# Graph network kernel: message types applied to a whole round of 16 groups at once, with VectorE's additions one round later

## What is computed

```python
h = jax.nn.relu(node_features @ node_proj_w.T + node_proj_b)
for l in range(L):                                   # L = 2
    trans = jnp.einsum('nh,tdh->tnd', h, edge_W[l])  # 8 types, 128 x 128 each
    msgs = trans[edge_type, src]
    agg = jax.ops.segment_sum(msgs, dst, num_segments=num_nodes)
    h = jax.nn.relu(_gru_cell(agg, h, gru_wih[l], gru_whh[l], gru_bih[l], gru_bhh[l]))
return h @ out_w.T + out_b
```

## Time and profile before

| | us |
|---|---|
| median of 3 runs | 2032.73 |
| lowest, highest | 2016.99, 2032.94 |
| profiled execution | 2030.53 |
| its span, first to last instruction | 2028.7 |
| mean granted clock | 0.897 of 2.4 GHz |
| PE busy | 1533.5 (76%) |
| POOL busy | 1189.5 (59%) |
| DVE busy | 809.0 (40%) |
| ACT busy | 500.7 (25%) |

### The profile page before, as it was taken

How to read it: one execution, slowest core, us unless ns; L and a number is a source line. 1 busy time by engine, 2 the same in 40 slices (tenths; PEclk the granted TensorE clock), 3 DMA queues, 4 the chain that set the end, 5 groups by cost and what they waited for, 6 DMA issues and landing times.

```text
span 2028.7 us, 32940 instructions
## 1 busy us (share of the span) xinstructions
PE 1533.5 (76%) x10492; PEld 1061.7 (52%) x10493; DVE 809.0 (40%) x3350; ACT 500.7 (25%) x958; POOL 1189.5 (59%) x1282
## 2 busy tenths in 40 slices
PE   5467888787778865777774888888887776677786
PEld 3345555454545544666562545555555445556565
DVE  6657262524323244454443222222523224444443
ACT  5233151514225112222221101111514211122221
POOL 7355666566556664666634666665665565566661
PEclk9679999899899977898987999989998987899998
DMA  6423727163462422222213776765243362222221
GB/s 165 125 58 110 238 85 269 54 235 118 137 201 68 136 75 65 80 78 78 76 50 103 257 239 226 257 217 152 68 133 88 90 170 64 68 75 71 75 76 32
DMA packets 183323, 251.61 MB, mean 124 GB/s; under 512 B 24396, under 2 KB 156641, under 8 KB 183201
## 3 DMA queue, kind: packets, MB, share of 16 engines
q1 hardware_dynamic: 123041, 130.73, 20.5%
q0 software_dynamic: 58176, 119.22, 20.3%
q10 hardware_dynamic: 1984, 0.13, 0.1%
HBM read 211.87 MB, written 38.12 MB: 123 GB/s over the span
## 4 chain that ended last, share of the span: by engine, by line
PE 39%; another core or an unknown queue 27%; issue 11%; DVE 10%; DMA 4%; ACT 4%; DVEq 3%; SPq 1%; POOL 1%; PEld 1%; ACTq 0%; PEldq 0%; POOLq 0%
PE ps L1070 11%; PE ps L1141 7%; PE ps L1047 7%; PE ps L1133 5%; PE ps L1008 4%; DMA blocks<-node_table 3%; PE ps L1121 3%; DVE acc L1653 2%; DVE onehot L1576 2%; ACT counts L775 2%; PE ps L1113 1%; ACT sums_sb L845 1%; PE ps L1086 1%; DVE acc L1673 1%
## 5 line engine op out<-in xcount | busy, mean ns | idle before, releaser
L587 POOL DMA_INDIRECT gath<-node_table,srcT x1212 | 1153.5, 952 | 793.2 <-issue 305.6
L1673 DVE TENSOR_TENSOR acc<-ps,acc 128x16 f32 x864 | 150.7, 174 | 785.3 <-remote 338.4
L1070 PE MATMUL ps<-counts,blocks 128*128 128x504 f16 (+3 forms) x1764 | 413.4, 381 | 63.9 <-issue 31.6
L845 ACT COPY sums_sb<-ps 128x512 f32<-128x512 f32 x216 | 126.2, 586 | 829.7 <-remote 514.6
L1070 PEld LDWEIGHTS ps<-counts,blocks 128*128 128x128 bf16 x1764 | 169.8, 100 | 257.6 <-issue 75.3
L1047 PE MATMUL ps<-work 128*128 128x392 bf16 x983 | 218.1, 357 | 110.2 <-ACT counts L775 43.6
L1141 PE MATMUL ps<-sums_sb,wT 128*128 128x128 f32 x1728 | 244.4, 299 | 65.2 <-ACT sums_sb L845 55.7
L1141 PEld LDWEIGHTS ps<-sums_sb,wT 128*128 128x128 f32 x1728 | 230.6, 212 | 82.9 <-DVE acc L1673 30.0
L1133 PE MATMUL ps<-onehot,gath 128*128 128x128 bf16 x2592 | 200.7, 228 | 59.3 <-issue 39.3
L1133 PEld LDWEIGHTS ps<-onehot,gath 128*128 128x128 bf16 x2592 | 174.8, 103 | 103.1 <-issue 66.0
L775 ACT CAST counts<-ps 128x392 f16<-128x392 f32 x429 | 187.7, 498 | 118.8 <-PE ps L1047 52.4
(11 more groups left out here) (199 smaller groups left out, 869.8 us busy)
## 6 DMA issues: line engine op xcount, KB each, us to landing
blocks<-node_table SPq DMA_DIRECT2D x84, 672.0 KB
kept_counts<-counts SPq DMA_DIRECT2D x28, 882.0 KB
counts<-kept_counts SPq DMA_DIRECT2D x28, 882.0 KB
gath<-node_table,srcT POOLq DMA_INDIRECT x1212
node_table<-gath SPq DMA_DIRECT2D x14, 336.0 KB, 3.2
node_table<-work SPq DMA_DIRECT2D x14, 336.0 KB
counts<-in_x_dram SPq DMA_DIRECT2D x1, 3080.0 KB
out_dram<-counts SPq DMA_DIRECT2D x13, 224.0 KB
```

The source lines that it names most:

```text
L587: nc.gpsimd.indirect_dma_start(out=gath[:, b, j, :], out_offset=None, in_=tables[l], in_offset=bass.IndirectOffsetOnAxis(ap=index, axis=0) ...
L845: act.copy(n_sb[:, b // 2, b % 2 * BG:(b % 2 + 1) * BG, :], narrow_sums[b % 2]) \
L1070: last = nc.tensor.matmul(head_ps[:, 0:COLS[share]], blocks[:, j % 2, at, part * H:(part + 1) * H], counts[:, a, 0:COLS[share]], start=(i ...
L1673: nc.vector.tensor_tensor(win, narrow_ps[q][:, g * NARROW:(g + 1) * NARROW], win, ALU.add) \
```

## The change

The types are applied less often, in wider products, and DVE's additions move.

- Narrow rounds: all four slots' sums are copied side by side into one place (`n_sb`, now a single place and not two halves), and `narrow_types` runs once, at the end of the round, with 256 columns. DVE makes the 16 additions at the start of the next round (`add_narrow(n - 1)`), before it writes one-hots; the one-hots of a slot now wait for `sums_ready` of that slot, and `make_hots` for the head stands behind the one-hots of slots 1 and 3.
- Wide rounds: a new `wide_types` covers two slots with 192 columns; it runs after slot 2's sum and after slot 3's. DVE adds 8 windows in a row (`add_wide`), then writes two slots' one-hots, then runs the tile's piece. `before_tanh` stands first in DVE's round.
- The short last round keeps `by_type`.

```diff
-        win_ps = [ps[:, 4 + b, 0:BG * WIN] for b in range(2)]
-        narrow_ps = [ps[:, 4 + q, 0:2 * BG * NARROW] for q in range(2)]
+        win_ps = [ps[:, 4 + q, 0:2 * BG * WIN] for q in range(2)]
+        narrow_ps = ps[:, 4, 0:ROUND * NARROW]
...
+                def wide_types(k, q):
+                    pe.wait_ge(es[l]["sums_copied"], k + (2 * q + 4))
+                    pe.wait_ge(es[l]["acc_added"], (k + 2) * BG)
+                    for t in range(T):
+                        last = nc.tensor.matmul(win_ps[q].rearrange("p (g w) -> p g w", g=2 * BG),
+                                                wT[:, W_EDGE + l * T + t, :],
+                                                s_sb[:, q, :, t * WIN:(t + 1) * WIN],
+                                                start=(t == 0), stop=(t == T - 1))
+                    last.then_inc(es[l]["win_done"], 2)
...
-                def narrow_types(k, q):
-                    pe.wait_ge(es[l]["sums_copied"], k + (2 * q + 4))
-                    pe.wait_ge(es[l]["acc_added"], (k + 2 * q) * BG)
+                def narrow_types(k):
+                    pe.wait_ge(es[l]["sums_copied"], k + (SLOTS + 2))
+                    pe.wait_ge(es[l]["acc_added"], (k + 2) * BG)
...
                     narrow_sums_of(k, landed, 2)
                     if head is None:
                         piece(pe, begin, gate_in, l + 1, tile)
-                    narrow_types(k, 0)
-                    if head is None:
                         piece(pe, begin, gate_z, l + 1, tile)
...
                     sum_by_code(k, landed, 0)
                     sum_by_code(k, landed, 1)
                     piece(pe, begin, gates_begin, k, tile)
-                    by_type(k, 0)
+                    sum_by_code(k, landed, 2)
                     piece(pe, begin, gate_in, l + 1, tile)
-                    sum_by_code(k, landed, 2)
-                    by_type(k, 1)
+                    wide_types(k, 0)
                     piece(pe, begin, gate_z, l + 1, tile)
                     sum_by_code(k, landed, 3)
-                    by_type(k, 2)
-                    by_type(k, 3)
+                    wide_types(k, 1)
                     piece(pe, begin, to_rows, l + 1, tile)
...
                 def narrow_round(n, head=None, last=False):
                     if head is None:
                         begin, tile = round_tile(dve, mybir.EngineType.DVE, n)
+                        add_narrow(n - 1)
+                    elif head > 0:
+                        add_narrow(n - 1, added_until(l, head))
                     k = n * SLOTS
+                    for b in range(SLOTS):
+                        dve.wait_ge(sem_l["sums_ready"], k + (b + 1 + SLOTS))
+                        (one_hots if last else narrow_hots)(n * ROUND + (ROUND + b * BG), b)
+                        if head is not None:
+                            if b % 2:
+                                for g in MADE[l].get(head + b - 1, []):
+                                    make_hots(g)
+                            head_slot(l, head + b, (k + 2) * BG)
+                        elif b == 1:
                             piece(dve, begin, before_tanh, l + 1, tile)
+                        elif b == 2:
                             piece(dve, begin, new_state, l + 1, tile)
+                        elif b == 3:
                             piece(dve, begin, state_parts, l + 1, tile)
```

More of the change, by code:

```diff
@@ L311, in gnn_kernel @@
         hots = onehot.rearrange("p b g c -> p (b g c)").bitcast(F32)
-        places = (one_half[0:ROWP, 0, 0:RC * GE], one_half[0:ROWP, 1, 0:RC * GE], hots[0:ROWP, 0:RC * GE])
+        places = (one_half[0:ROWP, 0:RC * GE], one_half[0:ROWP, RC * GE:2 * RC * GE], hots[0:ROWP, 0:RC * GE])
         dst_i, src_i, typ_i = (rows(t, I32) for t in places)
@@ L843, in narrow_round @@
                         act.wait_ge(es[l]["sums_ready"], k + (b + 1 + SLOTS))
[L844 to L845 removed]
+                        if b == 0:
+                            act.wait_ge(es[l]["win_done"], k + 2)
+                        act.copy(n_sb[:, b * BG:(b + 1) * BG, :], narrow_sums[b % 2]) \
                            .then_inc(es[l]["sums_copied"], 1)
@@ L1654, in add_windows, with add_wide @@
                           .then_inc(sem_l["acc_added"], 1)
-                def add_narrow(k, g0, q, after_head, hots):
-                    if len(hots) <= FIRST_HOTS:
-                        for g in hots:
-                            make_hots(g)
-                        hots = []
+                def add_wide(k, g0, q):
                     for half in range(2):
@@ L1680, in narrow_round @@
                         begin, tile = round_tile(dve, mybir.EngineType.DVE, n)
+                        add_narrow(n - 1)
+                    elif head > 0:
+                        add_narrow(n - 1, added_until(l, head))
                     k = n * SLOTS
[L1682 to L1693 removed]
+                    for b in range(SLOTS):
+                        dve.wait_ge(sem_l["sums_ready"], k + (b + 1 + SLOTS))
[6 more added lines that the diff above has]
+                        elif b == 1:
+                            piece(dve, begin, before_tanh, l + 1, tile)
+                        elif b == 2:
                             piece(dve, begin, new_state, l + 1, tile)
[L1695 removed]
+                        elif b == 3:
                             piece(dve, begin, state_parts, l + 1, tile)
```

89 lines of the change are left out of this document (43 added, 46 removed).

## The result

The changed kernel took 2050.24 us (median of 20 runs), the kernel before 2027.45 (20 runs): ratio 1.0124, 95% interval 1.0099 to 1.0149. It is slower by 1.2%, and inside the range of 1960 to 2085, but the forecast was "no change", 2026 us, and the time lies above the forecast's own range of 2005 to 2045. The profiled execution's span is 2047.2 us, 18.5 more than before.

A forecast was written before the change was run, and what follows sets the result against it. A signal loop of PE, POOL and ACT was taken as the bound. Head -29, narrow +18 and wide +4 gave -7 on 2030.5, 2023.5 us; 2.2 for the median made 2026. Own range 2005 to 2045, with rivals 1960 to 2085.

The forecast's parts named there:

- the charge for the late signal in the wide rounds: Wide rounds: new_state waits behind eight additions begun by a late first-types signal, charged 2.3 us a round.
- What bounds the kernel: All rounds: a loop of PE, POOL and ACT through signals; results during gather runs seen up to 5 us late.
- Head rounds, "I take -0.6, the work alone": 48 head rounds: one 256-column types call replaces two of 128, saving 0.6 us each, -29 us in all.
- the rule of the Trainium skill: Head types: loads priced at columns over 1.2 GHz, 107 ns; by it the change saves nothing, head term 0.
- Narrow rounds with a tile, "I take +3": Six narrow rounds with a tile: additions in line before the gates, less part of the types, +18 us in all.
- Wide rounds, +0.2: Twenty wide rounds: four parts sum to -2.1 us, against a late-signal charge of 2.3; +4 us in all.
- part (2): Wide rounds: before_tanh comes first on DVE, removing PE's wait before gate_z, -2.9 us a round.
- part (1): Wide rounds: two types calls of 192 columns replace four calls, 7.7 to 5.2 us, -2.5 us a round.
- the second: Slower rival, 2076 us: DVE becomes the spine of rounds with a tile, +2.5 us a wide round; chance 0.24.
- The first: Faster rival, 1967 us: loops loosen, one POOL idle per head round goes, wide rounds gain; -66 us, chance 0.33.
- The third: Slower rival, 2075 us: late head one-hots make PE wait about 3 us in 17 counting rounds, +51 us; chance 0.07.
- the bound of 1%: Whole kernel: chances of faster by over 1% 0.37, within 1% 0.31, slower 0.32.

The follow-up runs named there:

- the timely pair: Profiles of the kernel before and the changed kernel where signals are seen in time; head rounds 968.4 us before and 966.5 after.
- the other late job: Repeat of the changed kernel against the kernel before, with signals again seen late: ratio 1.0006, interval 0.9977 to 1.0036.
- the two halves: Only the narrow or only the wide half of the change, against the kernel before: timely 1.0028, 1.0030 and 1.0018, 1.0034; narrow late 0.9940, wide not met late.
- before_c: The kernel before, unchanged, profiled with signals seen in time: wide rounds 183.0 and 182.7 us, head rounds 968.4 us.
- after_c: The changed kernel, unedited, against the kernel before, with signals seen in time: 1657.89 us against 1635.04, ratio 1.0139.
- pool_pause_e: Changed kernel with POOL waiting for slot 1's gathers to land before slot 2's in wide rounds, against the kernel before, signals late: ratio 0.9983.

## Why the prediction was wrong, point by point

The step that failed is the charge for the late signal in the wide rounds: 2.3 us a round, where DVE saw the first types 8.5 us late and PE stood 7.83 us. The second step was the head: of the 29 us that PE's saved work was to bring there, little or nothing came.

- **What bounds the kernel**: right. Signals of PE that fall into a run of gathers are seen late, and a round is a loop over them. But I took the lateness as a constant, 3.05 us from one row. It depends on how many gathers still stand in line: reports deep in a run mostly wait for its end, those at its start hardly wait (last section). I also misread the run in the earlier trace rows as four gathers. The trace has eight in line there, 646.62 to 656.32 us.
- **Head rounds, "I take -0.6, the work alone"**: the row of 256 columns came as 3.72 us (3.5 forecast), so PE saves 0.4 us of work a round at the higher clock. The forecast 29 us are not there: the five late profiles with the changed head rounds have 1196 to 1203 us in them, both layers together, the two before 1201 and 1213, and the timely pair 966.5 and 968.4. What failed here is passing PE's work on to the round; this was a loop in which POOL or its signals end last, as the text itself said. The trace sides neither with my full 0.6 nor with nothing. By the rule of the Trainium skill ("TensorE: Matmul & The Clock Gate", section "LDWEIGHTS (loading the stationary operand)"), an estimate that the prediction worked out, the change would save nothing of 4.1 us; the trace has 0.4.
- **Narrow rounds with a tile, "I take +3"**: the additions took what was worked out, 5.6 us (5.4 forecast), but DVE began late, and the gates came 11.3 us behind the types (1714.99 to 1726.25) where 9 stood. The sum was of the wrong sign under late signals (-4.2 and -11.9 where +9 each stood). The later gates broke the runs of twelve; that this is what shortened the rounds is argued from the timeline, not tested. In the timely pair the stretches are equal (+0.1, +0.5), and the additions show up as backlog, paid at the layer's end.
- **Wide rounds, +0.2**: the price of a call was right at the higher clock (2.76 us, 2.6 forecast), and the wait before `gate_z` went, as part (2) said. The late signal, "I charge 2.3", was the step that failed: DVE saw the first types 8.5 us late, and PE stood 7.83 us before the second, which also ran at the lower clock, 4.91 us. With that, the two calls took 7.67 us and nothing was left of part (1), -2.5. And one edit had no term at all: the third sum's move ahead of `gate_in`. It is the one that fills POOL's run up to twelve, by the timeline. The earlier trace rows could have told it: 8.63 us of waiting and the lower clock stood there behind just such a run, though that round as a whole took only 24.0 us. A late job with the third sum put back was not met, so the move's own share stays unmeasured.
- **Rivals**: the second was nearest, slower, with its point of decision (the first types end inside a run) met in the eight wide rounds of layer 2 behind the first. Its size, 2.5 us a round, came as 3.0 in layer 2 and 0.8 in layer 1, and its narrow rounds were wrong. The first didn't happen. The third didn't either: PE waited 13.3 us in all for the count one-hots (L1047 behind L1540), and 12.8 before the change. Its sum was also off: 2030.5 + 51 - 5 is 2076.5, and not 2075.
- **Against the bound of 1%**: "within" had 0.31 and "slower" 0.32; it was slower, by 1.2%. By the other late job's 1.0006, it is luck on which side of the 1% one late job falls.

## What to carry to other kernels

Where several engines hand work on through signals, an edit that makes one of them faster also moves the moments at which it reports. Before costing the work saved, write down for each report in the loop what the receiver is in the middle of at that time, in the old and in the new order, and cost the moves that "only" change the order as well. When two edits cost nearly nothing alone because a buffer hides them, test them together: the buffer can be spent once. And run the pair in more than one job: here the two halves and the whole ranked differently by condition.

## What the runs showed of the hardware

What sets the timely profiles apart from the late ones is when signals are acted on. The gathers' group and the chain's shares of before_c:

```profile
L587 POOL DMA_INDIRECT gath<-node_table,srcT x1212 | 1157.9, 955 | 409.2 <-issue 360.7 <-DMA node_table<-work 23.4 <-DMA node_table<-gath 11.6
PE 35%; POOL 32%; issue 14%; DVE 9%; DMA 7%; DVEq 2%; ACT 1%; SPq 0%; ACTq 0%; POOLq 0%; PEldq 0%
```

A gather takes 0.955 us here and 0.952 in the earlier trace rows, but POOL's idle time is 409 us and not 793, and "another core or an unknown queue", 27% of the chain in the earlier trace rows, is absent. It has 24 to 33% of the chain in all seven late profiles and isn't named in any of the thirteen timely ones. The granted clock is higher too, 0.953 against 0.897, while PE stands idle less.

ACT's 304 copies of sums show the lateness as a whole. In the changed kernel's first profile (late), 228 could have begun inside a run of gathers, since the sum was done and ACT was free. Of these 131 did begin before the run's end, 86 of them within 0.5 us, and 97 only behind it. The place in the run decides: of those ready in its first 2 us (74) the median was 0.04 us late, of the 48 ready after 6 us or more 44 had to wait for the end. In after_c (timely) 293 were ready inside a run, and the median was 0.04 us late, the most 0.93. In after_c the z gate's products end at 1520.43, in the middle of POOL's gathers, and ACT starts on them 0.03 us later:

```profile
1519.51 0.92 PE L1008 MATMUL ps<-acc,wT 128*128 x2
...
1520.46 0.63 ACT L731 ACTIVATE work<-ps,brz 128x448 f32<-128x448 f32 x1 [4.01 <-PE ps L1008]
```

The same step took 6.9 us in the round shown at the top (1863.3 to 1870.20). In the timely condition the kernel before takes 1636 us and not 2027, a difference of 24% that no edit here comes near. The condition came and went between jobs on the same chip, and held for all executions of a job. What causes it, and why it strikes PE's signals while POOL issues gathers, no run here shows. Two of pool_pause_e's eleven executions took 3116 and 3579 us and are not in its ratio; nothing here explains these either.
